# Token mixing of the first two batches as seven products of halves, with the sums of quarters on GpSimd

## The chip, the cores and the metric

The kernel runs on one core of a Trainium2 chip. Its engines work side by side, each through its own list of instructions in order, and wait for each other on semaphores: TensorE (PE, with its weight loads shown as PEld), VectorE (DVE), ScalarE (ACT), GpSimd (POOL), and SyncE (SP), which issues the DMAs. The metric is the device time of one execution, in microseconds (us).

## The reference

One gated transformer block on four batches of 512 tokens of width 512, all in float32. The part that the change touches is the first line of the last two: the mixing of tokens by attention.

```python
query  = einsum('bnc,dc->bnd', ctx, Wq) + bq          # 4 x 512 x 128
key    = einsum('bnc,dc->bnd', ctx, Wk) + bk
P      = softmax(einsum('bnd,bmd->bnm', query, key))  # 4 x 512 x 512
x_m    = einsum('bln,bmn->blm', layernorm(x), P)      # 4 x 512 x 512
x = x + tanh(g_xattn) * x_m
x = x + tanh(g_ffn) * ffn(layernorm(x))   # ternary weights, 512 -> 2048 -> 512, silu gate
```

## The kernel before

The program is one straight list for each engine, written out by Python loops; no scheduler moves anything. It has two stages.

**Attention stage** (about 0 to 96 us). The loop runs over the batches b = 0 to 3 (the change's "batches one and two" are b = 0 and 1). While batch b is mixed, the scores of batch b + 1 are made. On TensorE a batch is: `project(b+1, 0)`, `transpose_p(b, 3)`, `project(b+1, 1)`, and then four calls of `mix(b, i)` (line 639), one for each tile i of 128 rows, with `energy(b+1, ..)` and `transpose_p(b+1, ..)` between them. `mix` multiplies a tile of x, which comes already transposed from DRAM (`xt_sb`), by the transposed attention matrix of the batch (`at_batch`, in `sh`): four products of 128 x 128 x 512 that add up in one PSUM bank. All of it is float32, and each such product is two instructions on TensorE in the trace. The layer norm of x is not applied ahead of the product: VectorE adds the PSUM tile, scaled by `tr1` (the row's 1/std times the gate), to x (`make_x1`, line 1338), and the constant part (`km1`) is added much later. `tr1` is worked out by GpSimd in four small dependent steps for each tile (`rstd1`, line 494) from statistics that VectorE makes (`stats1`, `aggregate1`). Then VectorE makes the statistics of the new x (`stats2`), GpSimd the 1/std (`rstd2`, line 503), and VectorE the normalised rows (`norm_x1`, line 1354).

ScalarE computes the exponentials (`exp_row`), their scaling (`norm_p`) and the copies of the transposed attention (`copy_at`), and between these it sums the absolute values of the weights as they come in (`sum_abs`). SyncE's list of DMAs is in order too: the transposed tiles of batch 1 (`load_xt(1, i)`, line 345) stand between the 1 MB loads of weights, and each waits until the tile of the batch before has been used.

**Feed-forward stage** (from 96 us). Here the products are already done as seven products of halves (`product`, line 708), in float16 pairs. Their operands are sums of halves of the normalised rows (`B11`, `B21`, `T1` to `T4`), made in the attention stage: `t3_sb` (line 1427) at the end of batch 1, the others in batches 2 and 3.

## Time and profile before

| | us |
|---|---|
| three timed runs, median | 398.37 |
| the three runs | 397.30, 398.42, 398.37 |
| span of the profiled execution | 397.2 |
| TensorE busy | 392.9 (99%) |
| VectorE busy | 309.2 (78%) |
| ScalarE busy | 266.6 (67%) |
| GpSimd busy | 153.5 (39%) |

The profile is of one execution, and its span runs from the first instruction to the last. What lies around the span is small: the shortest of the three timed runs is 0.1 us longer, the median 1.2 us. In the attention stage the DMA engines are busy all the time from 10 to 50 us, VectorE is between 50% and 90% busy, and GpSimd mostly waits.

### The profile page before, as it was taken

What the parts mean: (1) busy time and instruction counts of PE and PEld (TensorE: products, weight loads), DVE (VectorE), ACT (ScalarE), POOL (GpSimd) and SP (SyncE); (2) the same over time, 40 slices, a digit from 0 to 9 for tenths busy, and PEclk for the clock granted to TensorE, in tenths of its full rate; (3) what the DMA queues carried; (4) which work ended last, traced back from release to release, by engine and by line L of the source; (5) the groups of instructions that cost most, each with busy time, mean ns of one, the idle gap of its engine ahead of it and who ended that gap; (6) DMA issues with size and microseconds to landing.
All of it is one profiled execution on the core that took longest, in us unless ns stands there. A gap on an engine that the chain in (4) does not pass through costs nothing.

```text
span 397.2 us, 5960 instructions
## 1 busy us (share of the span) xinstructions
PE 392.9 (99%) x1912; PEld 207.6 (52%) x1920; DVE 309.2 (78%) x457; ACT 266.6 (67%) x360; POOL 153.5 (39%) x189
## 2 busy tenths in 40 slices
PE   8999999999999999999999999999999999999997
PEld 6555545554444444444444444444445565656886
DVE  0666578988889986788897966686869989798974
ACT  3886898889779686868887863756277666654400
POOL 0224344657985004131338001535349556271000
DMA  7999949599610030030009543041500000000014
GB/s 268 410 420 390 376 173 224 141 248 217 134 70 1 2 106 2 0 106 2 1 2 212 110 90 68 0 146 70 173 37 2 0 2 1 2 0 2 0 55 160
DMA packets 43183, 43.91 MB, mean 111 GB/s; under 512 B 30992, under 2 KB 33168, under 8 KB 41104
## 3 DMA queue, kind: packets, MB, share of 16 engines
q1 hardware_dynamic: 43152, 43.53, 35.7%
q8 instruction: 16, 0.26, 0.3%
q14 instruction: 15, 0.12, 0.1%
HBM read 29.89 MB, written 6.29 MB: 91 GB/s over the span
## 4 chain that ended last, share of the span: by engine, by line
PE 93%; DVE 2%; issue 2%; ACT 1%; DMA 1%; POOL 0%; DVEq 0%; ACTq 0%; POOLq 0%
PE pair L718 23%; PE pair L720 22%; PE pair L650 14%; PE pair L792 14%; PE pair L836 11%; PE pair L625 4%; PE pair L611 3%; PE pair L636 2%; PE pair L665 1%; DMA xf<-in_first 1%; DVE xf L1467 1%; DVE x_sb L1518 0%; PE pair L669 0%; POOL xf L588 0%; DVE xf L1457 0%
## 5 line engine op out<-in xcount | busy, mean ns | idle before, releaser
L718 PE MATMUL pair<-xb_hi,w_sb 128*128 128x512 f16 x448 | 169.8, 379 | 0.2 <-DVE xf L1462 0.2
L720 PE MATMUL pair<-xb_lo,w_sb 128*128 128x512 f16 x448 | 169.8, 379 | 0.0
L718 PEld LDWEIGHTS pair<-xb_hi,w_sb 128*128 128x128 bf16 x448 | 43.8, 98 | 52.8 <-ACT xf L1145 0.9
L720 PEld LDWEIGHTS pair<-xb_lo,w_sb 128*128 128x128 bf16 x448 | 43.8, 98 | 51.1 <-issue 0.3
L1096 ACT ACTIVATE xf<-xf,small 128x512 f32<-128x512 f32 x48 | 34.6, 720 | 52.3 <-DVE xf L1462 31.6
L650 PE MATMUL pair<-sh,xt_sb 128*128 128x512 f32 (+2 forms) x160 | 57.4, 508 | 0.0
L792 PE MATMUL pair<-x_sb,sh 128*128 128x512 bf16 x248 | 55.1, 379 | 0.4
L1467 DVE SCALAR_TENSOR_TENSOR xf<-xf,small 128x512 f32<-128x512 f32 x48 | 40.0, 835 | 8.4 <-ACT xf L1096 8.4
L650 PEld LDWEIGHTS pair<-sh,xt_sb 128*128 128x128 f32 x160 | 28.0, 190 | 26.2 <-issue 22.0
L792 PEld LDWEIGHTS pair<-x_sb,sh 128*128 128x128 f16 x256 | 24.9, 98 | 30.6 <-DVE x_sb L1504 0.9
L512 POOL TENSOR_TENSOR w_sb<-w_sb 128x512 bf16<-128x512 bf16 x8 | 9.6, 1196 | 63.0 <-ACT w_sb L970 63.0
L1472 DVE TENSOR_TENSOR sh<-xf,sh 128x512 f16<-128x512 f32 x36 | 32.1, 897 | 0.7 <-ACT sh L1107 0.7
L1518 DVE SCALAR_TENSOR_TENSOR x_sb<-pair,small,x_sb 128x256 f32<-128x256 f32 (+1 forms) x57 | 25.5, 473 | 5.9 <-PE pair L836 5.4
L1504 DVE SCALAR_TENSOR_TENSOR x_sb<-pair,small,x_sb 128x512 f32<-128x512 f32 x32 | 23.9, 746 | 7.9 <-PE pair L792 7.7
L1107 ACT ACTIVATE sh<-xf 128x512 f16<-128x512 f32 x36 | 22.1, 623 | 10.5 <-DVE xf L1467 9.3
L584 POOL TENSOR_TENSOR xf<-xf 128x512 f32<-128x512 f32 x7 | 9.8, 1405 | 44.7 <-DMA xb_lo<-xf 28.7
L1457 DVE TENSOR_TENSOR xf<-pair,xf 128x1024 f32<-128x1024 f32 x16 | 19.5, 1221 | 8.8 <-PE pair L720 8.6
L1452 DVE TENSOR_TENSOR xf<-pair,xf 128x1024 f32<-128x1024 f32 x16 | 19.5, 1220 | 4.1 <-issue 1.6
L1462 DVE TENSOR_TENSOR xf<-pair,xf 128x1024 f32<-128x1024 f32 x16 | 19.5, 1219 | 4.1 <-PE pair L720 3.9
L1133 ACT ACTIVATE xf<-pair 128x1024 f32<-128x1024 f32 x16 | 16.4, 1023 | 8.1 <-PE pair L720 7.6
L1341 DVE SCALAR_TENSOR_TENSOR x_sb<-pair,small,x_sb 128x512 f32<-128x512 f32 x16 | 12.0, 747 | 11.3 <-PE pair L650 11.3
L1467 DVE SCALAR_TENSOR_TENSOR c<-c,small,pair 128x512 f32<-128x512 f32 x16 | 11.9, 743 | 10.1 <-ACT c L1096 10.1
(162 smaller groups left out, 654.6 us busy)
## 6 DMA issues: line engine op xcount, KB each, us to landing
w_sb<-in_wugT SPq DMA_DIRECT2D x8, 1024.0 KB, 11.3
xt_sb<-in_xT SPq DMA_DIRECT2D x16, 256.0 KB, 6.4
x_sb<-in_x SPq DMA_DIRECT2D x4, 1024.0 KB, 10.8
xf<-in_wdT SPq DMA_DIRECT2D x4, 1024.0 KB, 7.3
xt_sb<-in_wdT SPq DMA_DIRECT2D x4, 1024.0 KB, 5.2
x_dram<-x_sb SPq DMA_DIRECT2D x8, 256.0 KB, 2.8
out<-x_sb SPq DMA_DIRECT2D x8, 256.0 KB, 2.0
x_sb<-x_dram SPq DMA_DIRECT2D x2, 1024.0 KB, 5.7
```

The costliest lines, as they stand in the source:

```text
L650: last = pe.matmul(ps_x[i % 2][:, lo:hi], xt_tile(i)[:, k, :], at[:, k, lo:hi], start=(k == 0), stop=(k == KD - 1))
L718: pe.matmul(dst[:, m * 512:(m + 1) * 512], w[:, o:o + P], hi[:, k], start=start and k == 0, stop=False, skip_group_check=not start)
L720: last = pe.matmul(dst[:, m * 512:(m + 1) * 512], w[:, o:o + P], lo[:, k], start=False, stop=k == 1, skip_group_check=not start)
L792: ins = pe.matmul(dst, h_part(n, c, lo)[:, i * P:(i + 1) * P], t_d[:, e * DM + lo_col:e * DM + hi_col], start=first and n == units[0] and ...
L836: ins = pe.matmul(fin_bank(g, j, t), hidden(u, c, lo, min(t, NT - 1)), cols, start=first and u == units[0] and lo == 0 and not (side and t ...
L1096: act.activation(cb(n, c)[:, 0:512], src, ACT.Silu, scale=su[:, :]).then_inc(s_silu[c], 1)
L1107: act.activation(part(n, c, 0), shaped(n, c, cb(n, c)[:, 0:512]), ACT.Copy).then_inc(s_hi[c], 1)
L1452: dve.tensor_tensor(cb(n, "11"), ps_y[:, :], cb(n, "11"), ALU.add).then_inc(s_c["11"], 1)
L1467: dve.scalar_tensor_tensor(cb(n, c)[:, 0:512], cb(n, c)[:, 0:512], kap[:, :], gate, ALU.mult, ALU.mult).then_inc(s_mul[c], 1)
L1472: dve.tensor_tensor(part(n, c, 1), shaped(n, c, cb(n, c)[:, 0:512]), part(n, c, 0), ALU.subtract)\
L1504: dve.scalar_tensor_tensor(y_tile(b, i), at, c_out[:, :], y_tile(b, i), ALU.mult, ALU.add)\
L1518: dve.scalar_tensor_tensor(fin_rows(g, j, t), fin_bank(g, j, t), c_out[:, :], fin_rows(g, j, t), ALU.mult, ALU.add).then_inc(s_ef, 1)
```

## The change

For b = 0 and 1 the four calls of `mix` become seven calls of `mix_product`. With the transposed x in four quarters (half of the rows lh, half of the tokens nh) and the attention in four quarters, each product multiplies one quarter (or a sum of quarters) by another: two row tiles times two pieces of 128 tokens, over 256 columns. That is 4 products of 128 x 128 x 256 for each of the seven, 28 for a batch, where there were 16 of 128 x 128 x 512. The order is 1, 5, 6, 3, 7, 2, 4. Products 1, 6, 7, 4 add up in one PSUM bank and 5, 3 in the other, so VectorE must have added a bank's contents to x (`add_mixed`, two instructions on 128 x 256) before the next product goes into it.

The sums of quarters are made by GpSimd: four of x (`x_sums`, after all four tiles of the batch have landed) and four of the attention (`p_sums_1`, `p_sums_2`, after its last piece has been copied). `rstd1` and `rstd2` handle two tiles at once in these batches (`rstd1_two` has five steps, `rstd2_two` two), and all of these stand in GpSimd's one list. The transposed tiles of batch 1 get a place of their own (`xb_lo`), so their loads wait for nothing. The row normalisation of batch 1 goes from VectorE to GpSimd, and `t3_sb` is made in batch 2, i = 0, instead of at the end of batch 1. The core of the diff:

```diff
             def load_xt(b, i):
-                if b > 0:
-                    sp.wait_ge(s_xm, (b - 1) * NT + i + 1)
-                sp.dma_start(xt_tile(i), xT[b, i]).then_inc(d_xt[i], 16)
+                if b == 2:
+                    sp.wait_ge(s_mp, 7)
+                elif b == 3:
+                    sp.wait_ge(s_xm, i + 1)
+                sp.dma_start(xt_tile(b, i), xT[b, i]).then_inc(xt_in(b, i)[0], 16)
...
+            def x_sums(b):
+                for i in range(NT):
+                    pool.wait_ge(*xt_in(b, i))
+                pool.tensor_tensor(x_sum(b, 0), x_quarter(b, 1, 0), x_quarter(b, 1, 1), ALU.add).then_inc(s_ss, 1)
+                hold(pool, s_ss, 4 * b + 1)
+                pool.tensor_tensor(x_sum(b, 1), x_sum(b, 0), x_quarter(b, 0, 0), ALU.subtract).then_inc(s_ss, 1)
+                hold(pool, s_ss, 4 * b + 2)
+                pool.tensor_tensor(x_sum(b, 2), x_quarter(b, 0, 1), x_sum(b, 1), ALU.subtract).then_inc(s_ss, 1)
+                pool.tensor_tensor(x_sum(b, 3), x_quarter(b, 0, 0), x_quarter(b, 1, 0), ALU.subtract).then_inc(s_ss, 1)
+
+            def p_sums_1(b):
+                hold(pool, s_at, b * NT + NT)
+                pool.tensor_tensor(p_sum(b, 0), p_quarter(b, 0, 1), p_quarter(b, 0, 0), ALU.subtract).then_inc(s_ts, 1)
+                hold(pool, s_ts, 4 * b + 1)
+                pool.tensor_tensor(p_sum(b, 1), p_quarter(b, 1, 1), p_sum(b, 0), ALU.subtract).then_inc(s_ts, 1)
...
-            rstd1(0, 0)
-            rstd1(0, 1)
-            for b in range(NB - 1):
+            x_sums(0)
+            rstd1_two(0, 0)
+            p_sums_1(0)
+            rstd1_two(0, 1)
+            p_sums_2(0)
+            x_sums(1)
+            rstd1_two(1, 0)
+            rstd2_two(0, 0)
+            rstd1_two(1, 1)
+            rstd2_two(0, 1)
+            p_sums_1(1)
+            p_sums_2(1)
+            rstd1(2, 0)
+            rstd1(2, 1)
+            for h in range(2):
+                rstd2_two(1, h)
+                norm_x1(1, 2 * h)
+                norm_x1(1, 2 * h + 1)
+            for b in range(NS, NB - 1):
...
+            def mix_product(b, j):
+                if j == 1:
+                    pe.wait_ge(s_at, b * NT + 2)
+                    pe.wait_ge(*xt_in(b, 0))
+                    pe.wait_ge(*xt_in(b, 1))
+                    if b > 0:
+                        pe.wait_ge(s_xe, 14 * b)
+                elif j != 5:
+                    pe.wait_ge(s_xe, added(b, {6: 1, 7: 6, 4: 7, 3: 5, 2: 3}[j]))
+                a, t = XA[j], PB[j]
+                if j in (5, 6, 3, 7):
+                    pe.wait_ge(s_ss, 4 * b + a + 1)
+                if j in (5, 6, 7, 4):
+                    pe.wait_ge(s_ts, 4 * b + t + 1)
...
+                if b < NS:
+                    mix_product(b, 1)
+                    energy(b + 1, 0)
+                    energy(b + 1, 1)
+                    mix_product(b, 5)
+                    mix_product(b, 6)
+                    transpose_p(b + 1, 0)
+                    energy(b + 1, 2)
+                    mix_product(b, 3)
+                    mix_product(b, 7)
...
+            for b in range(NS):
+                add_mixed(b, 1)
+                row_max(b + 1, 0)
+                row_max(b + 1, 1)
+                if b == 1:
+                    norm_x1(0, 2)
+                    norm_x1(0, 3)
+                row_rsum(b + 1, 0)
+                row_rsum(b + 1, 1)
+                add_mixed(b, 5)
...
+                    rows_in(1, 3)
+                    norm_x1(0, 0)
+                    norm_x1(0, 1)
...
                     if b == 2:
                         if i == 0:
+                            hold(dve, s_x2p, NT)
+                            dve.tensor_tensor(t3_sb, xf_half(1, 1), xf_half(1, 0), ALU.subtract).then_inc(s_t3, 1)
                             hold(dve, s_t3, 1)
```

The lists show where things stand now. First GpSimd's list at the start of batch 1, before: one round for one tile (L505 and L506 are `rstd2`, L497 to L500 `rstd1`), and such rounds follow each other through the whole stage.

```order
L505 TENSOR_SCALAR small<-small 128x1 [waits s_ln2]
L506 TENSOR_TENSOR small<-small 128x1 [waits s_pool]
L497 TENSOR_SCALAR small<-small 128x1 [waits s_ln1]
L498 TENSOR_TENSOR small<-small 128x1 [waits s_pool]
L499 TENSOR_TENSOR small<-small 128x1 [waits s_pool]
L500 TENSOR_SCALAR small<-small 128x1 [waits s_pool]
```

The same place after (a line number is of the changed kernel; `xb_lo` holds the transposed tiles, `xb_hi` the sums of x, `small` the statistics):

```order
L573 TENSOR_TENSOR xb_hi<-xb_lo 128x512 [waits d_xu2,d_xu3,d_xu1,d_xu0]
L575 TENSOR_TENSOR xb_hi<-xb_hi,xb_lo 128x512 [waits s_ss]
L577 TENSOR_TENSOR xb_hi<-xb_lo,xb_hi 128x512 [waits s_ss]
L578 TENSOR_TENSOR xb_hi<-xb_lo 128x512
L558 TENSOR_SCALAR small<-small 128x2 [waits s_ln1]
L559 TENSOR_TENSOR small<-small 128x2 [waits s_pool]
L560 TENSOR_SCALAR small<-small 128x2 [waits s_pool]
L561 TENSOR_TENSOR small<-small 128x2 [waits s_pool]
L562 TENSOR_SCALAR small<-small 128x2 [waits s_pool]
L567 TENSOR_SCALAR small<-small 128x2 [waits s_ln2]
L568 TENSOR_TENSOR small<-small 128x2 [waits s_pool]
```

After these comes a second pair of the same small groups, for tiles 2 and 3, and then the sums of the attention (L582 makes the one that product 5 needs):

```order
L567 TENSOR_SCALAR small<-small 128x2 [waits s_ln2]
L568 TENSOR_TENSOR small<-small 128x2 [waits s_pool]
L582 TENSOR_TENSOR xf<-sh 128x512 [waits s_at]
L584 TENSOR_TENSOR xf<-sh,xf 128x512 [waits s_ts]
L587 TENSOR_TENSOR xf<-sh 128x512
L589 TENSOR_TENSOR xf<-sh,xf 128x512 [waits s_ts]
L548 TENSOR_SCALAR small<-small 128x1 [waits s_ln1]
```

So four full-width sums and four groups of small steps stand between the landing of the tiles and the attention's first sum. TensorE's list at the start of the mixing of batch 1, before (L650 is `mix`, L625 `energy`, L636 `transpose_p`):

```order
L650 MATMUL pair<-sh,xt_sb 128x384 [waits s_x1,d_xt0,s_at]
L650 MATMUL pair<-sh,xt_sb 128x384 x3
L650 MATMUL pair<-sh,xt_sb 128x128 [waits s_at]
L650 MATMUL pair<-sh,xt_sb 128x128 x3
L625 MATMUL pair<-sh 128x512 [waits s_qk]
L625 MATMUL pair<-sh 128x512
L650 MATMUL pair<-sh,xt_sb 128x512 [waits s_x1,d_xt1]
L650 MATMUL pair<-sh,xt_sb 128x512 x3
```

And after (L786 is `mix_product`: product 1, two calls of `energy`, product 5, product 6):

```order
L786 MATMUL pair<-sh,xb_lo 128x256 [waits d_xu1,s_xe,d_xu0,s_at]
L786 MATMUL pair<-sh,xb_lo 128x256 x3
L736 MATMUL pair<-sh 128x512 [waits s_qk]
L736 MATMUL pair<-sh 128x512
L786 MATMUL pair<-xf,xb_hi 128x256 [waits s_ts,s_ss]
L786 MATMUL pair<-xf,xb_hi 128x256 x3
L786 MATMUL pair<-xf,xb_hi 128x256 [waits s_ts,s_ss,s_xe]
L786 MATMUL pair<-xf,xb_hi 128x256 x3
```

Product 5 has the first wait on GpSimd's sums (`s_ss` for x, `s_ts` for the attention). Last, VectorE's list from the end of batch 1 into batch 2, before (L1427 makes `t3_sb`, L1341 is `make_x1`, L1319 `row_max`):

```order
L1377 TENSOR_TENSOR xb_lo<-xf,xb_hi 128x1024 [waits s_th]
L1427 TENSOR_TENSOR t_sb<-xf 128x1024 [waits s_x2n]
L1341 SCALAR_TENSOR_TENSOR x_sb<-pair,small,x_sb 128x512 [waits s_r1,s_xm]
L1346 BN_STATS small<-x_sb 128x6 [waits s_x1]
L1319 TENSOR_REDUCE small<-pair 128x1 [waits s_e] x2
L1352 BN_AGGR small<-small 128x2 [waits s_bs]
L1330 BN_STATS small<-x_sb 128x6
L1323 RECIPROCAL small<-small 128x1 [waits s_exp] x2
L1336 BN_AGGR small<-small 128x2 [waits s_bs]
L1359 TENSOR_SCALAR xf<-x_sb,small 128x2x256 [waits s_abs,s_r2]
L1431 TENSOR_TENSOR xf<-xf 128x1024 [waits s_t3]
L1341 SCALAR_TENSOR_TENSOR x_sb<-pair,small,x_sb 128x512 [waits s_r1,s_xm]
```

And after (L1636 makes `t3_sb`, L1493 is `make_x1`, L1471 `row_max`):

```order
L1545 TENSOR_TENSOR xb_lo<-xf,xb_hi 128x1024 [waits s_th]
L1493 SCALAR_TENSOR_TENSOR x_sb<-pair,small,x_sb 128x512 [waits s_r1,s_xm]
L1513 BN_STATS small<-x_sb 128x6 [waits s_x1]
L1471 TENSOR_REDUCE small<-pair 128x1 [waits s_e] x2
L1519 BN_AGGR small<-small 128x2 [waits s_bs]
L1482 BN_STATS small<-x_sb 128x6
L1475 RECIPROCAL small<-small 128x1 [waits s_exp] x2
L1488 BN_AGGR small<-small 128x2 [waits s_bs]
L1527 TENSOR_SCALAR xf<-x_sb,small 128x2x256 [waits s_abs,s_r2]
L1636 TENSOR_TENSOR t_sb<-xf 128x1024 [waits s_x2p]
L1638 TENSOR_TENSOR xf<-xf 128x1024 [waits s_t3]
L1493 SCALAR_TENSOR_TENSOR x_sb<-pair,small,x_sb 128x512 [waits s_r1,s_xm]
```

The sum for `t3_sb` has moved from ahead of the first `make_x1` of batch 2 to ahead of the second.

## Rows read from the trace of the kernel before

**Rows 1.** The page, part 1: busy us (share of the span) and instructions.

```profile
PE 392.9 (99%) x1912; PEld 207.6 (52%) x1920; DVE 309.2 (78%) x457; ACT 266.6 (67%) x360; POOL 153.5 (39%) x189
```

**Rows 2.** Waits of TensorE over the whole span: who waited for whom, us, times, longest.

```profile
PE pair L661 <- POOL early L470: 1.0, 1, 1.0
PE pair L718 <- DVE xf L1462: 0.2, 1, 0.2
```

**Rows 3.** The chain that ended last: start us, us, engine, line, instructions.

```profile
18.07 3.47 PE pair L650 x16
21.54 1.72 PE pair L625 x4
23.26 3.43 PE pair L650 x8
26.70 0.44 PE pair L636 x4
...
36.60 1.72 PE pair L611 x4
...
63.04 3.47 PE pair L650 x16
```

**Rows 4.** The page, part 5: VectorE's additions of 128x256 from PSUM.

```profile
L1518 DVE SCALAR_TENSOR_TENSOR x_sb<-pair,small,x_sb 128x256 f32<-128x256 f32 (+1 forms) x57 | 25.5, 473 | 5.9 <-PE pair L836 5.4
```

**Rows 5.** SyncE's timeline: DMA issues of transposed tiles, start us, us.

```profile
2.58 2.18 SPq L348 DMA_DIRECT2D xt_sb<-in_xT  x4
...
36.63 0.33 SPq L348 DMA_DIRECT2D xt_sb<-in_xT  x1
```

**Rows 6.** Line L348 between 4.1 and 4.9 us: batch 0's last tile.

```profile
DMA to landing us min/median/max: 7.1/7.1/7.1
```

**Rows 7.** GpSimd's timeline: one tile's small steps and the next one's first.

```profile
16.80 0.19 POOL L497 TENSOR_SCALAR small<-small 128x1 f32<-128x1 f32 x1 [15.20 <-DVE small L1336]
17.14 0.56 POOL L498 TENSOR_TENSOR small<-small 128x1 f32<-128x1 f32 x1
17.84 0.19 POOL L499 TENSOR_TENSOR small<-small 128x1 f32<-128x1 f32 x1
18.20 0.27 POOL L500 TENSOR_SCALAR small<-small 128x1 f32<-128x1 f32 x1 [0.18 <-POOL small L499]
18.55 0.19 POOL L497 TENSOR_SCALAR small<-small 128x1 f32<-128x1 f32 x1
```

**Rows 8.** Line L584: GpSimd's sums of 128x512 float32, min/median/max ns.

```profile
L584 POOL TENSOR_TENSOR xf<-xf x7: 1266/1273/1710, 245.4 to 347.3; 128x512 f32<-128x512 f32 x7
```

**Rows 9.** ScalarE's timeline: start us, us, line, operation.

```profile
21.72 1.91 ACT L934 ACTIVATE xb_lo<-w_sb 128x2048 f16<-128x2048 f32 x1 [1.03 <-DMA w_sb<-in_wugT]
...
25.16 1.33 ACT L953 ACTIVATE sh<-sh,small 128x512 f32<-128x512 f32 x2
...
80.53 0.72 ACT L953 ACTIVATE sh<-sh,small 128x512 f32<-128x512 f32 x1
```

**Rows 10.** Line L348 between 36.6 and 36.9 us: batch 1's last tile.

```profile
DMA to landing us min/median/max: 4.4/4.4/4.4
```

**Rows 11.** Windows: length, busy of PE, PEld, DVE, ACT, POOL, clock, DMA, GB/s.

```profile
0.00:10.00 10.00, 8.98 (x31) 6.78 (x32) 0.35 (x1) 3.00 (x6) 0.97 (x11) 1.00 0.79 269
...
30.00:40.00 10.00, 10.00 (x34) 5.07 (x33) 6.93 (x17) 6.26 (x10) 4.59 (x15) 1.00 0.99 388
```

**Rows 12.** TensorE's timeline: start us, us, line, operation, count.

```profile
3.95 3.38 PE L665 MATMUL pair<-xf 128*128 128x256 f32 x8
7.17 1.90 PE L669 MATMUL pair<-xf 128*128 128x256 f32 x8
...
81.40 0.60 PE L636 MATMUL pair<-early,sh 128*128 128x128 f32 x4
```

**Rows 13.** VectorE's timeline: start us, us, line, operation.

```profile
71.03 1.22 DVE L1431 TENSOR_TENSOR xf<-xf 128x1024 f32<-128x1024 f32 x1
...
101.00 2.23 DVE L1377 TENSOR_TENSOR t_sb<-xf,t_sb 128x1024 f16<-128x1024 f32 x1 [1.22 <-ACT t_sb L989]
```

More of the change, by code:

```diff
@@ L36, in gated_block_kernel @@
     NWARM = 6
+    NS = 2
     FW = first.shape[2]
@@ L113, in gated_block_kernel @@
         d_xt = [sem(f"d_xt{i}") for i in range(NT)]
+        d_xu = [sem(f"d_xu{i}") for i in range(NT)]
         d_w = [[sem(f"d_w{m}{c}") for c in range(NABS)] for m in range(3)]
@@ L144, in gated_block_kernel @@
         s_half = sem("s_half")
+        s_ss, s_ts, s_mp, s_xe, s_x2p = (sem(n) for n in ("s_ss", "s_ts", "s_mp", "s_xe", "s_x2p"))
         s_dt, s_ev, s_shift = sem("s_dt"), sem("s_ev"), sem("s_shift")
@@ new lines, in rstd2_two @@
+            def rstd2_two(b, h):
+                two, own = slice(2 * h, 2 * h + 2), slice(b * NT + 2 * h, b * NT + 2 * h + 2)
+                hold(pool, s_ln2, b * NT + 2 * h + 2)
+                step(pool.tensor_scalar(ve2[:, two], mv2[:, own, 1], LN_EPS, 1.0 / XS ** 2, ALU.add, ALU.mult))
+                pool.tensor_tensor(r2[:, own], ve2[:, two], mhalf, ALU.pow).then_inc(s_r2, 2)
+            def x_sums(b):
[7 more added lines that the diff above has]
+                pool.tensor_tensor(x_sum(b, 3), x_quarter(b, 0, 0), x_quarter(b, 1, 0), ALU.subtract).then_inc(s_ss, 1)
@@ L503, in rstd2, with norm_x1 @@
+            def norm_x1(b, i):
+                hold(pool, s_r2, b * NT + i + 1)
+                g = b * NT + i
+                pool.tensor_scalar(xn_tile(b, i), rows(x_tile(b, i)), mv2[:, g, 0:1], r2[:, g:g + 1],
+                                   ALU.subtract, ALU.mult).then_inc(s_x2p, 1)
             def rstd2(b, i):
                 hold(pool, s_ln2, b * NT + i + 1)
[L505 to L506 removed]
+                g = b % 2 * NT + i
+                step(pool.tensor_scalar(ve2[:, i:i + 1], mv2[:, g, 1:2], LN_EPS, 1.0 / XS ** 2, ALU.add, ALU.mult))
+                pool.tensor_tensor(r2[:, g:g + 1], ve2[:, i:i + 1], mhalf[:, 0:1], ALU.pow).then_inc(s_r2, 1)
@@ L649, in mix @@
                     for k in range(KD):
-                        last = pe.matmul(ps_x[i % 2][:, lo:hi], xt_tile(i)[:, k, :], at[:, k, lo:hi],
+                        last = pe.matmul(ps_x[i % 2][:, lo:hi], xt_tile(b, i)[:, k, :], at[:, k, lo:hi],
                                          start=(k == 0), stop=(k == KD - 1))
                 last.then_inc(s_xm, 1)
+            def mix_product(b, j):
[12 more added lines that the diff above has]
+                    pe.wait_ge(s_ts, 4 * b + t + 1)
+                left = x_sum(b, a) if j in (5, 6, 3, 7) else x_quarter(b, *a)
+                right = p_sum(b, t) if j in (5, 6, 7, 4) else p_quarter(b, *t)
+                for i in range(2):
+                    for k in range(2):
+                        last = pe.matmul(mix_bank(j)[:, i * 256:(i + 1) * 256], left[:, i, k * P:(k + 1) * P], right[:, k, :],
+                                         start=j in (1, 5, 2) and i == 0 and k == 0, stop=k == 1, skip_group_check=True)
+                last.then_inc(s_mp, 1)
             def total(lo, hi, count, at):
@@ L688, in _ @@
                     project(b + 1, 1)
+                if b < NS:
[9 more added lines that the diff above has]
+                    if b == 1:
+                        pe.wait_ge(s_qk, 5)
+                        total(0, 2 * NABS, 2 * NABS, ps_q)
+                    transpose_p(b + 1, 1)
+                    energy(b + 1, 3)
+                    mix_product(b, 2)
+                    transpose_p(b + 1, NT - 2)
+                    mix_product(b, 4)
+                    continue
                 for i in range(NT):
@@ L692, in _ @@
                     mix(b, i)
-                    if b == 1 and i == 2:
-                        pe.wait_ge(s_qk, 5)
-                        total(0, 2 * NABS, 2 * NABS, ps_q)
                     if last:
```

154 lines of the change are left out of this document (118 added, 36 removed).

## The prediction

> **What bounds the kernel now.** I read the page first. Its part 1 says that TensorE is busy for 392.9 us of a span of 397.2 [rows 1]. Next come the waits of TensorE over the whole span: 1.0 us before its first instruction and 0.2 us later, nothing else [rows 2]. So TensorE is the bound everywhere. Two things can change the time: the work on TensorE's list, and new gaps in it. The chain of waits gives the price of each piece there, and the reader should see that the pieces touch: one call of `mix` 3.43 us (the first of a batch 3.47), two scores 1.72, one transpose 0.44, one projection half 1.72, and the mixing of batch 2 (the third) starts at 63.04 [rows 3].
>
> **What TensorE saves.** Four calls of `mix` cost 3.47 + 3 x 3.43 = 13.76 us. A product of 128x128x256 is half of one of 128x128x512, so one of the seven products (four of them) costs half a `mix`, 1.72 us, and seven cost 12.0. Two batches save 2 x 1.73 = 3.5 us. Nothing else leaves or enters TensorE's list.
>
> **Batch 0, second transpose group.** ScalarE sums weights until a load lands (it starts that sum only at 21.72, behind a DMA wait) and then does two exponentials and two scalings; the first scaling, which `transpose_p(1, 0)` needs, is the first half of the pair at 25.16, so it ends at 25.8 [rows 9]. Before, TensorE came to that transpose at 26.70 [rows 3]. Now it comes after product 1, two scores and products 5 and 6: 18.07 + 4 x 1.72 = 24.95. The loads ahead are the same, so ScalarE is not sooner, and TensorE waits 0.9 us. GpSimd's sums don't add to this. The fourth tile of x lands at 4.4 + 7.1 = 11.5 [rows 5, 6]; four sums of 128x512 in float32 take 1.27 each, if nothing disturbs them [rows 8], and are done by 17.1. The statistics of two tiles are there by 18.55 at the latest [rows 7]; five small steps (2.1 us, below) and one sum end at 21.9, and the next sum at 23.3. Product 5 wants the first at 21.5, product 6 the second at about 23.5: at most 0.4 us, inside the 0.9. From 25.9, the rest of the batch (0.44 + 0.86 + 3.44 + 0.44 + 0.86 + 1.72 + 0.44 + 1.72 = 9.9) ends at 35.8. VectorE's fourteen additions cost 0.47 us each [rows 4], so each pair is done within 1 us of its product, while two or more pieces of other work lie before the bank is wanted again.
>
> **Batch 1, product 5.** Projections and transpose (3.88), product 1 (1.72) and two scores (1.72) bring TensorE to product 5 at 43.1. It waits for `s_ts`, and GpSimd's list decides when that comes. The last transposed tile of batch 1 landed at 36.63 + 4.4 = 41.0 [rows 5, 10]. Its load now waits for nothing, but it stands behind the same megabytes of weights, and the DMA engines were 99% busy at 388 GB/s from 30 to 40 us [rows 11]: a load that queues earlier in a full queue lands at the same time. So `x_sums(1)` starts at 41.0. Four sums of 1.27 and two hand-overs of 0.15 make 5.4 us: 46.4. Then the small steps. A tile's four steps took 18.55 - 16.80 = 1.75 us before, the first 0.34, the power 0.70, the others 0.36 each [rows 7]; five steps are 2.1, and the two of `rstd2_two` 1.0. Two of each: 6.2 us, to 52.6. The first sum of the attention adds 1.27, and product 5 starts at 53.9 instead of 43.1: 10.8 us of an idle TensorE. VectorE can't run ahead meanwhile: `norm_x1(0, 0)` needs the first `rstd2_two`, at 49.5. What is late next lies behind it by less: `norm_x1(0, 2)` waits until 52.6 and holds two reciprocals and the addition of product 5, which isn't there before 55.7.
>
> From 53.9 the rest of the batch is 13.5 us (four products, 6.88; two transposes and scores, 2.6; two products and a transpose, 3.9; the weights' total, 0.1), and 3.88 more bring the mixing of batch 2 to 71.3, against 63.04: **8.3 us late**. As a sum: -3.5 + 0.9 + 10.8 = 8.2.
>
> **Batch 2, VectorE.** `t3_sb` costs 1.22 us, as its neighbour of the same shape does [rows 13], and now stands before the second `make_x1` of batch 2. There VectorE has no slack: the last scaling of batch 3's scores runs at 80.53 to 81.25 and TensorE takes its transpose at 81.40 [rows 9, 12]. That scaling follows the row maximum, which follows everything VectorE does in batch 2. So of 1.22 us all but 0.15 becomes a wait: **1.1 us**. GpSimd's four normalisations of batch 1 are not in the trace. They lie between nothing hidden and the longest full-width sum, 1.71 us each [rows 8]; I take 1.27, its median. With that they end before VectorE reaches `t3_sb`, some 8 us into the batch; at 1.71 they would end about 1 us later, still at about the time that they are wanted. Bounds for this paragraph: 0 to 2.4 (the sum twice over).
>
> **The clock after the gap.** The trace shows one change of TensorE's speed: eight instructions in 3.38 us soon after the start, and the same eight shapes in 1.90 us right behind them, from 7.17 [rows 12]. That is the step from 1.2 to 2.4 GHz, though the windows show 1.00 for the granted clock already there [rows 11]. TensorE had been idle before its first instruction; its work from 1.0 [rows 2] to 7.17 went at the slow level, so half of 6.2 us, 3.1, was lost. A gap of 10.8 us in the middle is something the trace doesn't have. Bounds: 0 if the clock stays, 3.1 if it has to come back as at the start. I take **3.1**, the only row there is for TensorE after a rest.
> The Trainium skill, "TensorE: Matmul & The Clock Gate", Part 1, says that an idle TensorE falls back to 1.2 GHz and needs sustained work to come back; by that rule the gap costs something, and the start of the trace agrees.
>
> **Sum.** 8.3 + 1.1 + 3.1 = 12.5 us on a span of 397.2: 409.7. The timed runs lie 0.1 to 1.2 us above the span, so I say **410 us**.
>
> **Rivals.**
> - *The clock stays at 2.4 GHz* over the gap. For it: the granted clock column shows 1.00 throughout. Against it: the slow first instructions. 397.2 + 8.3 + 1.1, and 0.5 around: 407.
> - *GpSimd is slower than its medians.* Sums of the same shape took up to 1.71 us [rows 8], and a sum of VectorE took 2.23 instead of 1.22 us while GpSimd worked beside it [rows 13]. Five sums in the chain at +0.44 are 2.2 us; two such collisions for VectorE in batch 2 add up to 1. That gives 413. Against it: VectorE is held by `norm_x1(0, 0)` while the first four sums run, so nothing disturbs them. The Trainium skill, "SBUF — State Buffer", Who interferes with whom, says that GpSimd and a VectorE instruction with two SBUF inputs exclude each other; this speaks for collisions around `t3_sb`, as the 2.23 us does.
> - *The saving stands: faster.* If the attention's first sum were ready when TensorE comes to product 5, only the 0.9 and 1.1 us would stand against 3.5: 395.7 + 0.5 = 396. The place is GpSimd's list at 41 us, the price 10.8 us, and it turns where the idle time before product 5 is 1.5 us, that is with the tiles landed by 31.7 us instead of 41.0 or GpSimd's 12.9 us of work cut to 3.6. The measured queue and the measured steps both stand against this.
> - *The small products gain nothing.* If products of 256 columns cost 10% more than half of one of 512, the saving is half gone, and the time is 411 to 412; the first `mix` of a batch, cut into 384 and 128 columns with twice the instructions, costs 3.47 instead of 3.43 us [rows 3], which speaks against it. It shifts the forecast by less than its range and goes with it.
> - *The two effects cancel*: a gap of 1.5 us, no change. It needs the same luck as the saving.
>
> **Chances.** Forecast (gap and slow clock) 0.62; clock stays 0.20; slower GpSimd 0.12; saving stands 0.04; cancel 0.02. Differences of about 0.3% (1.2 us) are what a measurement of this kernel can tell from none. Faster 0.04, same 0.02, slower 0.94. The lower end of the costs is 8.3 with nothing on top, 405.5, taken a little lower for loads that land up to half a microsecond sooner; the upper is 8.3 + 2.2 + 3.1 + 2.4 = 16.0, 413. The range is 405 to 413; it leaves out the saving and part of the slow case.
>
> **What would show it.** In the profile after: TensorE idle before the third group of products in batch 1 (the first with float32 operands in `xb_hi`), 10 to 12 us, ended by GpSimd's first attention sum; before it GpSimd busy without a break from 41 us; VectorE idle in front of `norm_x1` until about 49.5. The next eight instructions of TensorE take twice their 0.215 us if the clock fell. A second, small gap (0.9) stands at 25 us before a transpose, ended by ScalarE, and a third (1.1) before the last transpose of batch 2. The prediction is wrong if the tiles of batch 1 land long before 41 us, if GpSimd's full-width sums take under 1 us, or if the feed-forward stage, which I count as unchanged (its operands are as late as TensorE), has gaps of its own.

## The result

| us | before | after |
|---|---|---|
| median of the timed runs | 398.10 (4 runs, 397.30 to 398.42) | **412.48** (4 runs, 411.63 to 412.87) |
| span of the profiled execution | 397.2 | 410.5 |

The changed kernel is slower: ratio 1.036, 95% interval 1.034 to 1.038. The forecast was 410, range 405 to 413.

The profile after, as the page has it (parts 1, 2 and 4). It answers to [rows 1]:

```profile
PE 391.2 (95%) x1944; PEld 215.5 (52%) x1952; DVE 316.2 (77%) x473; ACT 267.3 (65%) x360; POOL 173.6 (42%) x189
...
PEclk9999669999999999999999999999999999999999
...
PE 76%; DMA 5%; DVE 5%; POOL 5%; issue 5%; ACT 2%; SPq 1%; DVEq 0%; POOLq 0%; ACTq 0%
```

TensorE has fallen from 99% to 95% of the span. Two slices of the clock row show 6; the page of before has no clock row, and its windows from 0 to 70 us all show 1.00. The chain that ended last now holds DMA and GpSimd. The waits of TensorE say where (engine and line, releaser, us in total, times, longest), against 1.0 and 0.2 in [rows 2]:

```profile
PE pair L786 <- POOL xf L582: 11.9, 1, 11.9
PE pair L747 <- ACT sh L1105: 2.4, 3, 1.2
PE pair L797 <- POOL early L521: 1.0, 1, 1.0
PE pair L747 <- DVE sh L1557: 0.5, 1, 0.5
PE pair L870 <- DVE xf L1669: 0.2, 1, 0.2
```

And TensorE's timeline after (start, us, line, operation, in brackets the idle time ahead and who ended it). L786 is `mix_product`, L763 `mix`, L747 `transpose_p`, L736 `energy`:

```profile
7.72 3.67 PE L736 MATMUL pair<-sh 128*128 128x512 f32 x8
...
14.96 0.66 PE L747 MATMUL pair<-early,sh 128*128 128x128 f32 x4 [0.54 <-DVE sh L1557]
...
17.17 1.89 PE L786 MATMUL pair<-sh,xt_sb 128*128 128x256 f32 x8
...
20.61 3.62 PE L786 MATMUL pair<-xf 128*128 128x256 f32 x16
24.51 0.66 PE L747 MATMUL pair<-early,sh 128*128 128x128 f32 x4 [0.28 <-ACT sh L1105]
...
38.38 1.89 PE L786 MATMUL pair<-sh,xb_lo 128*128 128x256 f32 x8
40.11 1.88 PE L736 MATMUL pair<-sh 128*128 128x512 f32 x4
53.91 6.06 PE L786 MATMUL pair<-xf,xb_hi 128*128 128x256 f32 x16 [11.93 <-POOL xf L582]
...
73.80 3.63 PE L763 MATMUL pair<-sh,xt_sb 128*128 128x384 f32 x16
...
89.81 0.66 PE L747 MATMUL pair<-early,sh 128*128 128x128 f32 x4 [1.20 <-ACT sh L1105]
...
94.84 0.65 PE L747 MATMUL pair<-early,sh 128*128 128x128 f32 x4 [0.94 <-ACT sh L1105]
95.33 10.51 PE L763 MATMUL pair<-sh,xt_sb 128*128 128x384 f32 x32
```

The pieces of before that answer to these, beside [rows 3, 12] (L625 is `energy`, L650 `mix`):

```profile
9.02 3.67 PE L625 MATMUL pair<-sh 128*128 128x512 f32 x8
...
17.91 3.63 PE L650 MATMUL pair<-sh,xt_sb 128*128 128x384 f32 x16
...
40.31 2.10 PE L650 MATMUL pair<-sh,xt_sb 128*128 128x384 f32 x6
...
62.88 3.63 PE L650 MATMUL pair<-sh,xt_sb 128*128 128x384 f32 x16
...
81.84 10.51 PE L650 MATMUL pair<-sh,xt_sb 128*128 128x384 f32 x32
```

The 16 instructions of products 5 and 6 take 3.62 us in batch 0 and 6.06 in batch 1, behind the gap. The windows (length, busy of PE, PEld, DVE, ACT, POOL, clock, DMA share, GB/s) show the clock at 0.56 of full speed there, which is the 1.2 GHz level for most of the stretch:

```profile
40.00:50.00 10.00, 1.99 (x6) 0.65 (x4) 0.80 (x2) 3.05 (x4) 8.14 (x13) 0.75 1.03 406
50.00:60.00 10.00, 6.09 (x18) 4.96 (x19) 6.78 (x13) 5.88 (x9) 7.18 (x12) 0.56 0.31 112
60.00:70.00 10.00, 10.00 (x51) 8.17 (x50) 8.25 (x22) 6.45 (x13) 2.18 (x7) 1.00 0.05 10
```

The gap from the inside. First the load of batch 1's last tile, as the chain has it: issued at 21.53, landed at 40.2. Then the timeline of GpSimd, which works without a break from 40.39 on (four of its 20 rows):

```profile
21.53 18.70 DMA xb_lo<-in_xT
```

```profile
40.39 1.27 POOL L573 TENSOR_TENSOR xb_hi<-xb_lo 128x512 f32<-128x512 f32 x1 [13.97 <-DMA xb_lo<-in_xT]
...
44.42 1.26 POOL L578 TENSOR_TENSOR xb_hi<-xb_lo 128x512 f32<-128x512 f32 x1
...
51.84 0.70 POOL L568 TENSOR_TENSOR small<-small 128x2 f32<-128x2 f32 x1
52.51 1.26 POOL L582 TENSOR_TENSOR xf<-sh 128x512 f32<-128x512 f32 x1
```

In batch 2 it is GpSimd's row normalisations of batch 1 (line L594: times, min/median/max ns) that hold VectorE:

```profile
L594 POOL TENSOR_SCALAR xf<-x_sb,small x4: 2075/2078/2094, 72.1 to 79.6; 128x512 f32<-128x512 f32 x4
```

```profile
82.80 0.55 DVE L1527 TENSOR_SCALAR xf<-x_sb,small 128x512 f32<-128x512 f32 x1 [1.27 <-POOL small L601]
83.27 1.22 DVE L1636 TENSOR_TENSOR t_sb<-xf 128x1024 f32<-128x1024 f32 x1
```

`rstd2(2, 0)` stands behind the last normalisation on GpSimd's list and is done at 82.7, so `norm_x1(2, 0)` waits 1.27 us, and `t3_sb` (1.22) comes behind it. Together they are the 2.6 us by which VectorE's second `make_x1` of batch 2 is late: it starts 11.93 us after the mixing does, against 9.29 before.

**The account of the two profiled executions**, from the starts of the same pieces in both timelines:

| | measured | predicted |
|---|---|---|
| TensorE's clock rises earlier after the start (7.72 against 9.02) | -1.30 | 0 |
| 7.72 to 17.17, against 9.02 to 17.91: VectorE's scaling late | +0.56 | 0 |
| batch 0: 21.21 against 22.40, of which 1.73 are saved | -1.73 + 0.54 | -1.73 + 0.9 |
| batch 1: 35.42 against 22.57: saved, gap, slow clock | -1.73 + 11.93 + 2.65 | -1.73 + 10.8 + 3.1 |
| batch 2: 21.53 against 18.96 | +2.57 | +1.1 |
| batch 3 and feed-forward | -0.2 | 0 |
| sum | +13.3 | +12.5 |

The rows are not independent. The tiles' landing and GpSimd's list set the start of product 5 at 53.91, whenever TensorE comes to it: what TensorE gains or loses ahead of it (the first three rows and the saving of product 1) only makes the gap longer or shorter. The 2.65 us behind the gap are mostly the 16 instructions of products 5 and 6, 6.06 - 3.62 = 2.44.

Each execution's time is 1.8 us above its own span in all the runs of both kernels (412.31 beside 410.5; 397.69 beside 395.9). So the profiled execution of before, with a span of 397.2, must have taken 399.0, 0.9 more than its median, and its clock rose late (at 7.17, against 5.86 to 7.25 in the other traces). Medians differ by 14.4 us, spans by 13.3; most of the difference is this scatter.

### The profile page after: what moved, and what is told of

The parts are those of the page before. It is cut to its first block, busy times and chain, and to the rows that moved or that the text cites. A ratio compares the mean times of both kernels' runs of the same rounds, so it can differ in the third digit from the quotient of the medians.

```text
span 410.5 us, 6058 instructions
## 1 busy us (share of the span) xinstructions
PE 391.2 (95%) x1944; PEld 215.5 (52%) x1952; DVE 316.2 (77%) x473; ACT 267.3 (65%) x360; POOL 173.6 (42%) x189
## 4 chain that ended last, share of the span: by engine, by line
PE 76%; DMA 5%; DVE 5%; POOL 5%; issue 5%; ACT 2%; SPq 1%; DVEq 0%; POOLq 0%; ACTq 0%
PE pair L870 22%; PE pair L872 22%; PE pair L944 13%; PE pair L988 11%; DMA xb_lo<-in_xT 5%; PE pair L763 3%; PE pair L786 2%; POOL xf L594 1%; DVE small L1471 1%; DMA xf<-in_first 1%; POOL small L568 1%; PE pair L736 1%; DVE xf L1674 1%; ACT sh L1100 1%; SPq L400 1%
## 5 line engine op out<-in xcount | busy, mean ns | idle before, releaser
L944 PEld LDWEIGHTS pair<-x_sb,sh 128*128 128x128 f16 x256 | 24.8, 98 | 30.7 <-DVE x_sb L1711 0.9
L1711 DVE SCALAR_TENSOR_TENSOR x_sb<-pair,small,x_sb 128x512 f32<-128x512 f32 x32 | 23.9, 747 | 7.8 <-PE pair L944 7.7
L763 PE MATMUL pair<-sh,xt_sb 128*128 128x512 f32 (+2 forms) x80 | 28.6, 508 | 0.0
L1100 ACT ACTIVATE sh<-pair,small 128x512 f32<-128x512 f32 x16 | 10.9, 683 | 15.2 <-DVE small L1471 15.1
L763 PEld LDWEIGHTS pair<-sh,xt_sb 128*128 128x128 f32 x80 | 13.9, 190 | 12.6 <-issue 10.5
L1674 DVE SCALAR_TENSOR_TENSOR c<-c,small,pair 128x512 f32<-128x512 f32 x16 | 11.9, 742 | 10.1 <-ACT c L1248 10.1
```

Source lines behind the costliest of these rows:

```text
L763: last = pe.matmul(ps_x[i % 2][:, lo:hi], xt_tile(b, i)[:, k, :], at[:, k, lo:hi], start=(k == 0), stop=(k == KD - 1))
L944: ins = pe.matmul(dst, h_part(n, c, lo)[:, i * P:(i + 1) * P], t_d[:, e * DM + lo_col:e * DM + hi_col], start=first and n == units[0] and ...
L1674: dve.scalar_tensor_tensor(cb(n, c)[:, 0:512], cb(n, c)[:, 0:512], kap[:, :], gate, ALU.mult, ALU.mult).then_inc(s_mul[c], 1)
L1711: dve.scalar_tensor_tensor(y_tile(b, i), at, c_out[:, :], y_tile(b, i), ALU.mult, ALU.add)\
```

## The experiments

The theory is the prediction's: (1) the last tile of batch 1 lands at 40 us, and behind it stand 12.9 us of GpSimd's work ahead of the first attention sum; (2) the gap that follows drops TensorE's clock; (3) GpSimd's normalisations and `t3_sb` delay batch 2. The rival for (1) was that sums are slow or the saving small; for (2) that the clock stays; for (3) that `t3_sb` alone does it. All kernels are the changed one with the edit shown, run against the kernel before (median 398.1).

**e1, small steps ahead of the sums of x** (batch 1, GpSimd).

```diff
-            x_sums(1)
             rstd1_two(1, 0)
             rstd2_two(0, 0)
             rstd1_two(1, 1)
             rstd2_two(0, 1)
             p_sums_1(1)
+            x_sums(1)
             p_sums_2(1)
```

> GpSimd's list in batch 1: the small steps and the first two attention sums stand ahead of the sums of x. Nothing else differs from the changed kernel. Theory A (the wait is the order: work that needs only VectorE and ScalarE results queued behind tiles that land at 40.4): product 5 waits only for the tiles and one sum, until about 43.1 instead of 53.9, TensorE is idle about 1.1 us there instead of 11.9, the clock stays, and the time is 412.5 - 10.8 - 2.6 = 399.1. Theory B (GpSimd simply has too much work in batches 0 and 1): the same work in another order moves the wait to product 6, 3 or 7, and the time stays above 408.

Measured 405.5, ratio 1.018 (1.017 to 1.020). Seven of the fourteen microseconds are gone, but the time is 6.4 us above what theory A gave. Product 5 waits 4.3 us, now for the first sum of x, and products 5 and 6 take 5.41 us. GpSimd's timeline shows why:

```profile
39.38 0.36 POOL L558 TENSOR_SCALAR small<-small 128x2 f32<-128x2 f32 x1 [2.28 <-DVE small L1488]
...
42.92 1.26 POOL L582 TENSOR_TENSOR xf<-sh 128x512 f32<-128x512 f32 x1
...
45.55 1.45 POOL L573 TENSOR_TENSOR xb_hi<-xb_lo 128x512 f32<-128x512 f32 x1
```

VectorE has the statistics of batch 1's last tile only at 39.2 us, the attention's sums stand behind the small steps that need them, and the sums of x, whose tiles had landed at about 41, stand behind the attention's. So the order inside this list counts as well as its length.

**e2, batch 1's tiles loaded ahead of the weights** (SyncE).

```diff
             load_ctx(2)
-            load_ug(0, 3)
-            load_ug(1, 0)
             for i in range(NT):
                 load_xt(1, i)
-                if i < 3:
-                    load_ug(1, i + 1)
+            load_ug(0, 3)
+            for i in range(NT):
+                load_ug(1, i)
```

> The four transposed tiles of batch 1 are loaded ahead of the five remaining 1 MB weight loads; GpSimd's list stays as in the changed kernel. Theory A (late tiles at the head of a serial list): the tiles land near 28, the sums of x are done by about 33, the small steps follow VectorE's statistics, product 5 starts near 43 and the time is about 399. If the late landing were harmless and the chain of GpSimd's steps the whole cause, product 5 would still start at 53 or later and the time would stay at 412.

Measured 400.6, ratio 1.006 (1.005 to 1.008). Moving one group of loads takes back 11.9 of the 14.4 us. Product 5 now waits for 1.55 us

```profile
45.01 3.69 PE L785 MATMUL pair<-xf,xb_hi 128*128 128x256 f32 x16 [1.55 <-POOL xf L581]
```

and runs with product 6 in 3.69 us. The sums of x are done at 33.7; what is left ahead of product 5 is the same wait for statistics as in e1. Elsewhere TensorE still waits 2.2 us in batch 2, as in the changed kernel, and 1.0 us ahead of batch 0's transposes.

**e3, the gap filled with idle products.** The 12 products go into a bank that nobody reads.

```diff
                     energy(b + 1, 1)
+                    if b == 1:
+                        for _ in range(12):
+                            pe.matmul(ps_k, ones[:, :], k_sb, start=True, stop=True)
                     mix_product(b, 5)
```

> Twelve float32 products of 128x128x512 whose result nobody reads (10.3 us of TensorE, into a free PSUM bank) stand in the gap ahead of product 5 of batch 1. Clock theory: products 5 and 6 ran at 1.2 GHz only because TensorE had rested; kept busy until about 52.3, it runs them in 3.4 instead of 6.1 us, and the time is 412.5 - 2.6 = 409.9. Rival (products 5 and 6 are slow since their operands are being written or read by GpSimd and VectorE at the time): they stay at 6 us and the time at 412.5.

Measured 410.9, ratio 1.032 (1.031 to 1.034). TensorE's timeline:

```profile
42.59 10.46 PE L831 MATMUL pair<-sh,early 128*128 128x512 f32 x24
54.56 3.69 PE L786 MATMUL pair<-xf,xb_hi 128*128 128x256 f32 x16 [1.51 <-POOL xf L582]
```

Products 5 and 6 take 3.69 us instead of 6.06, with the gap as long as before. That is the clock's share, 2.4 us in the trace, 1.6 in the medians. Product 5 itself began 0.65 later in this execution, since the tiles landed 0.6 later (GpSimd's first sum of x starts at 40.98 instead of 40.39). The expected time was 409.9.

**e4, batch 1's normalisations back on VectorE**, `t3_sb` at the end of batch 1.

```diff
 (GpSimd)
             for h in range(2):
                 rstd2_two(1, h)
-                norm_x1(1, 2 * h)
-                norm_x1(1, 2 * h + 1)
...
 (VectorE, end of batch 1)
+                    norm_1(0)
+                    norm_1(1)
                     low_t(0, "B21", xf_half(0, 1))
+                    norm_1(2)
+                    norm_1(3)
+                    hold(dve, s_x2p, NT)
+                    dve.tensor_tensor(t3_sb, xf_half(1, 1), xf_half(1, 0), ALU.subtract).then_inc(s_t3, 1)
...
 (VectorE, batch 2, i = 0)
-                            hold(dve, s_x2p, NT)
-                            dve.tensor_tensor(t3_sb, xf_half(1, 1), xf_half(1, 0), ALU.subtract).then_inc(s_t3, 1)
```

> The row normalisation of batch 1 is VectorE's again, and the sum into t3_sb stands at the end of batch 1, in the 3.2 us in which VectorE waits for the first product of batch 2. Theory: the two waits of TensorE in batch 2 (1.2 and 0.9 us ahead of transposes) and a little behind them come from these two moves alone, and go; 412.5 - 2.5 = 410.0. Rival (they come from batch 3's scores running later after the gap): no change, 412.5.

Measured 410.4, ratio 1.030 (1.029 to 1.032): 2.1 us less, where I expected 2.5. The two waits of 1.20 and 0.94 us in batch 2 are gone but for 0.29 us; the gap (11.5) is still there. The edit moves the normalisations and `t3_sb` at once, so it does not part them; that `t3_sb` alone is not the whole follows from VectorE's 1.27 us of waiting ahead of it, shown above, and no run tests it by itself.

**e7, two sums of 128x512 more** on GpSimd, between the landing and the gap.

```diff
+                for _ in range(2 * b):
+                    step(pool.tensor_tensor(x_sum(b, 3), x_quarter(b, 0, 0), x_quarter(b, 1, 0), ALU.subtract))
                 pool.tensor_tensor(x_sum(b, 3), x_quarter(b, 0, 0), x_quarter(b, 1, 0), ALU.subtract).then_inc(s_ss, 1)
```

> The changed kernel with the fourth sum of x of batch 1 made three times instead of once: 2 x 1.27 us of work and two hand-overs of 0.15 more in GpSimd's list ahead of product 5. If that list sets the start of product 5, the product starts 2.8 us later and the time is 412.5 + 2.8 = 415.3. If the wait ends with something else (the tiles, VectorE), less than 1 us is seen.

Measured 414.8, ratio 1.043 (1.041 to 1.045), 2.3 more than the changed kernel. Product 5 starts at 56.98 instead of 53.91. Of these 3.07 us, 0.24 are the tiles, which landed later in this execution (the first sum of x starts at 40.63); from there to product 5 it is 16.35 us instead of 13.52, 2.83 more, as expected (2.8). The work on GpSimd is worth its full length there. The time grew by less, since products 5 and 6 took 5.35 us this time instead of 6.06; why the slow stretch is sometimes shorter (5.20 us in e4) these runs don't show.

**e5 and e6, both cures together.** e5 is e2 and, on GpSimd, `p_sums_1(1)` ahead of `rstd1_two(1, 1)`; e6 is e5 and e4.

```diff
             rstd1_two(1, 0)
             rstd2_two(0, 0)
+            p_sums_1(1)
             rstd1_two(1, 1)
             rstd2_two(0, 1)
-            p_sums_1(1)
             p_sums_2(1)
```

> Two edits on the changed kernel: the tiles of batch 1 are loaded ahead of five weight loads, and the first two attention sums of batch 1 stand ahead of the small steps of its tiles 2 and 3, whose statistics VectorE makes last (near 39.5). Order theory: with only the loads moved, product 5 started at 45.0, behind those small steps; now its sum can start when ScalarE's last copy is there, near 38.5, and product 5 waits for nothing. 400.6 - 1.6 of idle time - 0.2 of slow clock = 398.8. Rival (what is left of the wait is GpSimd's throughput): another product or transpose of batch 1 waits instead and the time stays at 400.6.

> The edits of the run before, and also batch 1's row normalisation back on VectorE with the sum into t3_sb at the end of batch 1. If the two groups of waits are independent, 398.8 - 2.1 = 396.7, which is 1.4 below the kernel before (398.1). If VectorE, which has only 3.2 us free at the end of batch 1 in the changed kernel and less here, becomes late for the first additions of batch 2, the time stays near 398.

e5 measured 402.3, ratio 1.010 (1.009 to 1.012); e6 399.5, 1.004 (1.002 to 1.005). Both miss by 3 us, and e5 is slower than e2, which it was to improve. Product 5 waits for nothing now, but a wait came up behind it; first TensorE, then VectorE in e5:

```profile
43.40 3.62 PE L785 MATMUL pair<-xf,xb_hi 128*128 128x256 f32 x16
49.10 0.66 PE L746 MATMUL pair<-early,sh 128*128 128x128 f32 x4 [2.08 <-ACT sh L1104]
```

```profile
45.41 2.81 DVE L1526 TENSOR_SCALAR xf<-x_sb,small 128x512 f32<-128x512 f32 x2 [1.11 <-POOL small L567]
48.14 0.21 DVE L1474 RECIPROCAL small<-small 128x1 f32<-128x1 f32 x2
```

`norm_x1(0, 2)` and `(0, 3)` stand ahead of the reciprocals that ScalarE's scaling needs. They wait 1.11 us for `rstd2_two(0, 1)`, which the edit moved back, and take 2.81 us for two instead of 1.00, because GpSimd's sums run beside them (that this is the reason, e11 and e12 show below for the same kind of operation). In batch 2 TensorE's wait behind GpSimd's normalisations has grown too, from 1.2 us in e2 to 2.0 in e5. e6 against e5, 2.7 us, is again the price of the normalisations.

**e8, the attention's sums earlier, with the loads as in the changed kernel** (e5 without e2).

> The changed kernel with only the first two attention sums of batch 1 moved ahead of one pair of small groups (3.3 us). Order theory: product 5 starts 3.3 us earlier, near 50.5; but the 1/std of batch 0's tiles 2 and 3 come 2.7 us later, VectorE's normalisations with them, and the first transpose of batch 2's scores then waits up to 1 us: 412.5 - 3.3 + 1 = 410.2. Without that second effect 409.2; if the order were indifferent, 412.5.

Measured 413.6, ratio 1.039 (1.037 to 1.041), 3.4 above what I expected and 1.1 above the changed kernel. From GpSimd's first sum of x to product 5 it is 10.1 us instead of 13.5, so the order is worth the 3.4 us that I expected. But the same wait as in e5 follows, now 2.5 us, and with the clock still low: the four transpose instructions take 1.12 us instead of 0.66. From product 5 to the mixing of batch 2 it takes 24.0 us instead of 19.9. (In this execution the tiles also landed 1.7 us later than in the changed kernel's, so the gap is 9.2 and not 7.5.)

```profile
52.17 6.02 PE L786 MATMUL pair<-xf,xb_hi 128*128 128x256 f32 x16 [9.17 <-POOL xf L582]
60.67 1.12 PE L747 MATMUL pair<-early,sh 128*128 128x128 f32 x4 [2.48 <-ACT sh L1105]
```

**e9 and e10, VectorE's order.** e9 is e6, e10 is e5, each with

```diff
-                if b == 1:
-                    norm_x1(0, 2)
-                    norm_x1(0, 3)
                 row_rsum(b + 1, 0)
                 row_rsum(b + 1, 1)
                 add_mixed(b, 5)
+                if b == 1:
+                    norm_x1(0, 2)
+                    norm_x1(0, 3)
```

> e6 with one thing moved on VectorE: in batch 1 the row normalisations norm_x1(0,2) and norm_x1(0,3) stand behind row_rsum(2,0), row_rsum(2,1) and add_mixed(1,5) instead of ahead of them. Theory (queue order and two engines at once): in e6 TensorE's transpose of batch 2's scores waited 2.1 us at 48.16 for ScalarE's scaling, which waited for the reciprocals, which stood behind two normalisations of together 2.81 us (1.00 when GpSimd is still) and their 1.11 us wait. Moved, the reciprocals come at about 45.1, the transposes wait for nothing and TensorE's waits fall from 4.2 to about 2.1 us: 399.5 - 2.1 = 397.4 us (396.5 to 398.2), about 0.998 of the kernel before. Rival: ScalarE's scaling is late for its own queue's sake (the sums of absolute values ahead of it), or the normalisations only pass their wait on to the sums of product 5 and so to product 3: then 399 to 400 us and the wait shows at another line.

> e5 with the same move as in e9 (the normalisations of batch 1 stay on GpSimd). If the 2.1 us wait of e5 is VectorE's order, 402.25 - 2.1 = 400.2 us (399.5 to 400.9), with the waits of 1.2 and 0.9 us in batch 2 still there; e10 less e9 is then again the price of the normalisations on GpSimd, 2.7 us as between e5 and e6. Rival: the time is 402 us again, if the transpose waits for ScalarE anyway.

e9 measured 396.8 (12 runs, 395.9 to 397.5), ratio **0.997 (0.996 to 0.998)**: faster than the kernel before by 1.3 us, 0.3%. e10 measured 399.4, 1.004 (1.002 to 1.005), 2.9 below e5 (expected 2.1): the wait of 2.08 us is gone, and the one of 1.99 us in batch 2 has fallen to 1.56. e9's waits of TensorE:

```profile
PE pair L744 <- DVE sh L1560: 1.2, 2, 0.8
PE pair L794 <- POOL early L520: 1.0, 1, 1.0
...
```

From the first mixing (18.45) to batch 2's (60.52) e9 takes 42.07 us against 44.97: 2.9 of the 3.5 us are there. But the medians differ by 1.3 only, and the first row of the waits says where the rest is: transposes of batch 0 that wait for VectorE's scaling of the attention rows, before 17 us.

**e11 and e12, the first 17 us.** e11 is e9 with one wait; e12 lets the first sum of x through, waits, and reorders the rest of batch 0's list (and takes `row_max(1, 0)`, `(1, 1)` ahead of `add_mixed(0, 1)` on VectorE; the comments in the cut are mine):

```diff
 (e11)
+            pool.wait_ge(s_pn0, 3)
             x_sums(0)
 (e12)
-            x_sums(0)
+            x_sums_1(0)        # x_sum 0, wait_ge(s_pn0, 3), x_sum 1
+            p_sum_first(0)
             rstd1_two(0, 0)
-            p_sums_1(0)
+            p_sum_second(0)
             rstd1_two(0, 1)
+            x_sums_2(0)        # x_sum 2, x_sum 3
             p_sums_2(0)
```

> e9 with one wait more: GpSimd begins batch 0's sums of x only when VectorE has done its three scalings of attention rows (128x512 float32 each). Theory (two engines at once, already in the first 17 us): in the kernel before, GpSimd was idle there and the three scalings took 0.49 us each; in the changed kernels its sums run from 10.4 to 15.9 us and the scalings take 0.49 to 1.33 us, so TensorE's transposes of batch 0 wait 0.5 to 1.2 us for them (e9: 0.41 and 0.76). With the wait the three take 0.49 each again and those waits are gone; the price is known: the sums start at about 14.8 instead of 10.4, the first sum of the attention ends at 23.9, and product 5 of batch 0, due at 20.7, waits 3.2 us. Time: 396.8 - 1.2 + 3.2 = 398.8 us (398 to 400). Rival: the scalings are long for a reason of their own (ScalarE's exponentials beside them, or the memory of a DMA); then they stay at 0.5 to 1.3 us, and the time is about 400 us.

> e9 with batch 0's list on GpSimd in another order: the first sum of x at once (it ends before the first scaling of VectorE), then the wait for the three scalings, then the second sum of x, the first of the attention, the small steps, the attention's second, the small steps, and the third and fourth sum of x, which products 3 and 7 need only from 26 us on; VectorE takes the two row maxima of batch 1 ahead of adding product 1, since that addition now waits for the small steps to about 20 us. Theory: the scalings take 0.49 us, TensorE's 1.2 us of waits before 17 us are gone, and no product waits instead; but ScalarE's scaling of batch 1's scores isn't sooner than 25.0, so the transposes at 24.15 wait about 0.7 us: 396.8 - 1.2 + 0.7 = 396.3 us (395.6 to 397). Rival: the waits only move (product 6 on the addition of product 1, product 7 on the third sum of the attention): 397 us or more.

VectorE's three scalings in e9, GpSimd's sums beside them, and then the scalings in e11:

```profile
12.03 1.33 DVE L1560 TENSOR_SCALAR sh<-sh,small 128x512 f32<-128x512 f32 x1
...
14.14 0.63 DVE L1560 TENSOR_SCALAR sh<-sh,small 128x512 f32<-128x512 f32 x1
...
15.14 1.04 DVE L1560 TENSOR_SCALAR sh<-sh,small 128x512 f32<-128x512 f32 x1
```

```profile
11.81 1.27 POOL L574 TENSOR_TENSOR xf<-xf,xt_sb 128x512 f32<-128x512 f32 x1
13.22 1.27 POOL L576 TENSOR_TENSOR xf<-xt_sb,xf 128x512 f32<-128x512 f32 x1
14.45 1.45 POOL L577 TENSOR_TENSOR xf<-xt_sb 128x512 f32<-128x512 f32 x1
```

```profile
12.61 0.49 DVE L1561 TENSOR_SCALAR sh<-sh,small 128x512 f32<-128x512 f32 x1
...
13.89 0.48 DVE L1561 TENSOR_SCALAR sh<-sh,small 128x512 f32<-128x512 f32 x1
...
14.88 0.49 DVE L1561 TENSOR_SCALAR sh<-sh,small 128x512 f32<-128x512 f32 x1
```

With GpSimd still, they take 0.49 us each and the waits on them are gone, in e12 as well. So the collision is shown. In e9 each scaling ends 0.28 us after the sum beside it (13.08 and 13.36, 14.49 and 14.77, 15.90 and 16.18): the scaling that starts during a sum is held until the sum ends. e11 pays for it with the expected gap (3.4 us before product 5 of batch 0): 399.8, ratio 1.006 (1.004 to 1.009). Its runs fall into two groups, 398.9 to 399.8 (7) and 402.2 to 402.9 (5). The five have a mean granted clock of 0.991, the seven 0.996 to 1.0, so TensorE's clock was low for part of the five. The likely reason is that the rest of 3.4 us sometimes costs the clock and sometimes not; the one trace is of the first group, so this is not shown. e12 measured 396.7 (396.1 to 397.3), ratio 0.996 (0.995 to 0.997), which its interval doesn't part from e9. It was to gain 0.5 and gained 0.1: the 1.2 us come back as 0.5 at the transposes of batch 1, which ScalarE releases only at 24.8, which leaves 0.9 us less from the first scores to the mixing of batch 2 (51.49 us against 52.36). In the medians only 0.1 of it shows; in e12's trace the part after that is 0.6 us longer, and no run shows why. (In the profiled executions the clock rose between 5.9 and 7.3 us.)

## Why the prediction was right, and where its steps were off

- **TensorE saves 3.5 us: right.** From the start of one product to that of the next it is 1.73 us (25.86 to 27.59 to 29.32), so seven take 12.1, where four calls of `mix` took 13.8: 1.7 a batch.
- **The tiles of batch 1 land no sooner though their load queues earlier: right.** The last was issued 15 us earlier (21.53 against 36.63) and landed at 40.2 instead of 41.0. That 0.8 us is inside the scatter: in the traces of e1, e3, e4, e7 and e8, with the same order of loads, it landed between 40.5 and 42.0. e2, where the tiles landed by 27.7, shows that the queue in front was the cause.
- **GpSimd's chain of 12.9 us: right to 0.6.** It ran 13.5 us, from 40.39, where I had 12.9 from 41.0; that the two differences cancel is luck. Product 5 started at 53.91, as said; the gap is 1.1 us longer than predicted because TensorE was there earlier in this execution (0.7 us from its early clock less the scalings, 0.4 from the smaller wait at batch 0's transpose). e7 shows that it is this chain.
- **The clock: right.** I had taken 3.1 us from the start of the program; it was 2.65 in this trace, 2.44 of it in products 5 and 6, and e3 gives 2.4. My rival, that the clock stays, fell.
- **Batch 0's second transpose: 0.5 instead of 0.9.** TensorE came to it 0.9 us sooner than I had said, ScalarE's scaling 1.4 sooner (at 23.74 instead of 25.16), as the weight load ahead of it landed 1.2 sooner in this execution (its sum starts at 20.51 instead of 21.72).
- **Batch 2: the step that failed.** "With that they end before VectorE reaches `t3_sb`" rested on 1.27 us for a normalisation, the duration of a two-input sum. It takes 2.08, above even the bound of 1.71 that I had given: the range of rows was of another operation. So `rstd2(2, 0)` came late and VectorE waited 1.27 us ahead of `t3_sb`: 2.57 instead of 1.1 us. e4 gives 2.1 of it back. The Trainium skill, "GPSIMD Engine Reference", 4.1 Engine selection, has one-input work on GpSimd at roughly line rate and two-input work at about half of VectorE's speed; by it the normalisation would have been the quicker of the two. L594 at 2.08 and L573 at 1.27 us say the opposite for this form with two scalars per row.
- **The start: a step I left out.** I wrote of batch 0 that GpSimd's sums "don't add to this". They lie beside VectorE's scalings, from 10.3 to 16.0 us, and cost TensorE 0.56 us in the changed kernel, 1.4 in e9 (10.29 against 8.89 us for the stretch). In the changed kernel the gap ahead of product 5 swallowed this, so the time does not contain it; it counts in e2, e5, e6, e9 and e10, where the gap is small or gone. The Trainium skill, "SBUF — State Buffer", Who interferes with whom, says that a `tensor_scalar` of VectorE in a two-port mode and a GpSimd instruction exclude each other, the later one blocking whole; the trace agrees as far as the blocking goes, 0.49 against up to 1.33 us in e9, though no row names the mode. I had weighed that section for `t3_sb` alone.
- **Around the span**: I took 0.1 to 1.2 us, since I compared times with the span of an execution that was not among them; it is a constant 1.8. The forecast span was 409.7 and the measured one 410.5. As product 5 started where I had said, those 0.8 us all lie behind it: batch 2 1.5 more, the slow clock 0.45 and the last row 0.2 less. The other 1.5 us to the 412.3 of that execution are this constant, where my 410 had 0.3. The miss in batch 2 is the only one of mechanism that reached the time.
- **The break-even: wrong.** I had written that the change turns where product 5 waits 1.5 us. In e2 it waits 1.55, and the kernel is still 2.5 us slower than before: batch 2 costs 2.6 us instead of 1.1, and the scalings of the first 17 us, which I had at nothing, 1.3.
